# Second attention of a two-layer block: where TensorE's unread products stand, and how wide they are

## The reference

```python
def _L1_xattn_ref(q, k, v, gamma):          # q = layernorm(x), k = v = ctx, all [32, 64, 256]
    qh = q.reshape(B, 8, 8, 256)            # the 64 rows are split in 8 heads of 8 rows
    kh = k.reshape(B, 8, 8, 256)
    vh = v.reshape(B, 8, 8, 256)
    qk = jnp.einsum('bhdq,bhdl->bhql', qh, kh) * scale      # 256 x 256 scores for each head
    sm = jax.nn.softmax(qk, axis=-1)
    ret = jnp.einsum('bhql,bhdl->bhdq', sm, vh)
    return gamma * ret.reshape(B, 64, 256)
x = x + tanh(g_xattn[1]) * _L1_xattn_ref(layernorm(x), ctx, ctx, gamma)
```

## Time and profile before

| what | value |
|---|---|
| median of 3 runs | 708.63 us (707.40 to 709.66) |
| profiled execution: own time, span | 710.47 us, 708.7 us |
| PE busy over the span | 626.2 us (88%) |
| DVE, ACT, POOL busy | 501.0, 422.5, 283.4 us (71%, 60%, 40%) |
| PE in 360 to 370 us, inside the 15 steps | 9.59 of 10 us busy, granted clock 1.00 |

### The profile page before, as it was taken

One profiled execution on the slowest core, in us unless ns is written; L12 is line 12 of the kernel. 1 busy time (PEld: TensorE's weight loads), 2 busy tenths in 40 slices (PEclk: granted clock), 3 DMA queues, 4 the chain that ended last, 5 costly groups with the idle time before them and its releaser, 6 DMA issues. The chain is left out here.

```text
span 708.7 us, 16712 instructions
## 1 busy us (share of the span) xinstructions
PE 626.2 (88%) x5047; PEld 456.8 (64%) x5047; DVE 501.0 (71%) x885; ACT 422.5 (60%) x859; POOL 283.4 (40%) x385
## 2 busy tenths in 40 slices
PE   3788869999999758999999999999859889999995
PEld 2676747788888655444444444444457779999874
DVE  3878784788887965788888888788427744444656
ACT  3888864434343513888888888888825325555430
POOL 2455544222223453444434443453243624214254
PEclk9999987999999965999999999999959979999998
DMA  5444449000000043344333443342000236546444
GB/s 157 113 111 127 132 141 324 19 1 1 0 0 21 4 137 107 96 114 129 112 104 107 122 118 108 101 120 60 2 0 33 93 103 193 162 128 193 120 135 126
DMA packets 70369, 70.42 MB, mean 99 GB/s; under 512 B 10420, under 2 KB 66580, under 8 KB 70324
## 3 DMA queue, kind: packets, MB, share of 16 engines
q1 hardware_dynamic: 65092, 55.55, 26.7%
q0 software_dynamic: 5232, 14.29, 6.7%
HBM read 38.22 MB, written 31.33 MB: 98 GB/s over the span
## 5 line engine op out<-in xcount | busy, mean ns | idle before, releaser
L1375 DVE TENSOR_REDUCE a_smax<-a_s 128x4 f32<-128x1024 f32 x128 | 153.7, 1208 | 38.9 <-PE a_s L1307 37.6
L1189 ACT ACTIVATE a_prob<-a_st 128x512 f32<-128x512 f32 x256 | 144.1, 596 | 38.8 <-PE a_st L1302 37.5
L1302 PEld LDWEIGHTS a_st<-qop,kop 25*128 25x128 f32 x512 | 60.9, 185 | 71.3 <-issue 54.8
L1307 PE MATMUL a_s<-kop,qop 24*128 24x256 f32 x512 | 99.9, 339 | 7.4 <-DVE a_smax L1375 5.0
L1302 PE MATMUL a_st<-qop,kop 25*128 25x256 f32 x512 | 100.3, 330 | 6.6 <-ACT a_prob L1189 5.7
L1246 PE MATMUL a_pv<-a_prob,a_vt 128*32 128x256 f32 x1024 | 81.6, 391 | 2.2 <-ACT a_pv_sb L1174 0.7
L806 POOL TENSOR_TENSOR f_hs_lo<-f_kept,f_hs_hi 128x512 fp32r<-128x512 f32 x32 | 41.3, 1323 | 89.1 <-ACT f_hs_hi L756 89.1
L1307 PEld LDWEIGHTS a_s<-kop,qop 24*128 24x128 f32 x512 | 60.3, 190 | 9.8 <-DVE a_smax L1375 6.3
L1820 POOL DMA_INDIRECT sorted_rows<-m_xn,m_slot x32 | 32.9, 1029 | 49.5 <-PE m_gu L126 26.7
L124 PE MATMUL f_bank<-f_xt_hi,w_hi 128*128 128x512 f32 x128 | 51.6, 403 | 1.1 <-DVE w_raw L849 0.6
L125 PE MATMUL f_bank<-f_xt_lo,w_hi 128*128 128x512 f32 x128 | 50.8, 397 | 0.0
(11 more groups left out here) (260 smaller groups left out, 1700.7 us busy)
## 6 DMA issues: line engine op xcount, KB each, us to landing
kop<-kop_rows SPq DMA_DIRECT2D x128, 48.0 KB
qop<-qop_rows SPq DMA_DIRECT2D x128, 48.0 KB
sorted_rows<-x_all SPq DMA_DIRECT2D x2, 2944.0 KB, 15.4
expert_rows<-turned SPq DMA_DIRECT2D x46, 128.0 KB
kop_rows<-k_hi SPq DMA_DIRECT2D x32, 128.0 KB, 2.3
qop_rows<-q_hi POOLq DMA_DIRECT2D x30, 128.0 KB, 2.4
qop<-sorted_rows SPq DMA_DIRECT2D x24, 128.0 KB, 2.2
kop<-sorted_rows SPq DMA_DIRECT2D x22, 128.0 KB, 2.5
```

Source lines behind the costliest of these rows:

```text
L1189: act.activation(prob[:, u % 8], st_ps[u % 2][:], ACT.Exp, scale=SCALE1).then_inc(prob_ready, 1)
L1302: st = pe.matmul(st_ps[u % 2][:, c * D:(c + 1) * D], lhsT=kop[t.slot][strip, u // 4, c * P:(c + 1) * P], rhs=qop[t.slot][strip, u // 4], s ...
L1307: sm = pe.matmul(s_ps[j % 2][:, k, c * D:(c + 1) * D], lhsT=qop[v.slot][strip, w // 4, c * P:(c + 1) * P], rhs=kop[v.slot][strip, w // 4], ...
L1375: dve.tensor_reduce(smax[:, v.slot, opposite(2 * j):opposite(2 * j) + 2].rearrange("p u q -> p (u q)"), s_ps[j % 2][:].rearrange("p u (q n ...
```

## The change

Four lone products of 512 columns in each of the 15 steps go. In their place stand one such product, ahead of unit 6 behind its waits, and three pairs of products of 256 columns, each right ahead of two transposes (behind u = 2, 11 and 14), behind the waits of these transposes. The pairs write `misc[:, 256:512]`, the half that `selected` fills at u = 8 and ACT copies before u = 11. The number of unread columns of a step stays 4 x 512 = 2048 = 512 + 6 x 256.

```diff
-        EVERY = 4
+        SPARE = 6
...
-                def spare(u):
-
-                    pe.matmul(s_ps[j % 2][:, 0], lhsT=kop[v.slot][:, u // 4, 0:P],
-                              rhs=kop[v.slot][:, u // 8 * 2:u // 8 * 2 + 2].rearrange("p g n -> p (g n)"), start=True, stop=True)
+                def spare(count=2):
+
+                    if v.inside(TILES) and t.inside(TILES):
+                        for g in range(count):
+                            pe.matmul(misc[:, D:2 * D], lhsT=kop[v.slot][:, g % 2, 0:P], rhs=kop[v.slot][:, g % 2], start=True, stop=True)
+
+                def spare_scores():
+
+                    if v.inside(TILES) and t.inside(TILES):
+                        pe.matmul(s_ps[j % 2][:, 0], lhsT=kop[v.slot][:, 0, 0:P],
+                                  rhs=kop[v.slot][:, 0:2].rearrange("p g n -> p (g n)"), start=True, stop=True)
...
-                    if v.inside(TILES) and t.inside(TILES) and u % EVERY == 0:
-                        spare(u)
+                    if u == SPARE:
+                        spare_scores()
...
                     if u == 2:
-                        turn(t, 1, lambda: after(pe, vt_ready, t))
+                        def before():
+                            after(pe, vt_ready, t)
+                            spare()
+                        turn(t, 1, before)
...
                             after(pe, neg_t_ready, t, 2)
                             after(pe, back_ready, o)
+                            spare()
                         turn(v, 0, before)
...
                             pe.wait_ge(vt_cleared, 2)
+                        spare()
                         for c in range(DC):
                             mm = pe.transpose(misc[:, c * P:(c + 1) * P], ctx_t[:, v.slot, c * P:(c + 1) * P], ident[:])
```

## The result

The changed kernel takes 710.09 us (median of 11 executions, 708.72 to 710.80), the kernel before, in the same comparison, 708.27 us (11 executions): ratio 1.0023, 95% interval 1.0014 to 1.0033. It is 1.8 us slower, where 2.4 us less was forecast. Both ratios lie within the 0.3% that the prediction called no change, and both intervals exclude a gain. Three executions that spent far more time at the lower clock than the rest of their kernel (728.09 us of the kernel before, 798.15 us of e6_none, 723.40 us of e8_u12_only) are left out of the ratios.

The account below looks back on a forecast made before the run. PE was taken as the longest engine, each step a chain of its work and ACT's turn-around. Steps of 14.23 against 14.37 us save 2.1 us, the first step 0.3 more: 706.2 us from 708.63, range 702.5 to 711.5.

Parts of the forecast that it names:

- section 1: Transposes at u = 11, or the pair ahead of them, to unit 14: from 1.81 to 2.05 us, +0.24.
- A pair therefore costs 2 x 0.12 = 0.24 beside transposes: PE's price for each new pair beside transposes: 0.24 us, or at most 0.43 if it paid its own change.
- sign of being wrong towards slower: In PE's timeline, a pair with its transposes at over 0.65 us in place of 0.55.
- The sum: Four sections of a step add up to 14.23 us against 14.37, so -0.14 a step.
- sections 3 and 1: Section 3 is unit 2 to unit 6: from 3.44 to 3.68 us, +0.24; section 1 has its own line.
- section 2: Unit 14 to unit 2 of the next step: from 3.50 to 3.31 us, -0.19.
- The delay on ACT: At u = 11, ACT's work queued behind the transposes moves by 0.24 us; neg_t copied 0.66 behind the pair's first product.
- The clock phases in other stages, which I take as unchanged: Outside the changed stage, clock phases stay; they account for 1 us either way.
- No change to speak of: Rival, chance 0.18: small term errors use up the step's saving of 0.14 us; 707.5 to 709.5 us.
- The pairs pay their own change: Rival, chance 0.15: each of three pairs costs 0.19 to 0.20 us more; +0.44 a step, 715.2 us.
- The clock falls: Rival, chance 0.05: PE's clock falls between unit 6 and u = 11; 2 us a fall, 738 us if every step.
- PE's work is what counts: Rival, chance 0.15: ACT's turn-around shrinks and PE's whole saving of 0.38 us a step comes; 702.9 us.

Follow-up runs that it names:

- e6_none: Changed kernel without any unread product in the steps, except the 18 in the first; 702.66 us, ratio 0.9781 to the kernel before.
- e8_u12_only: Kernel before with only the lone product at u = 12 left of its four; 705.46 us, ratio 0.9799.
- e3_behind: Changed kernel with three products of 512 columns right behind the transposes instead of the pairs ahead; 705.20 us, ratio 0.9947 to the kernel before.
- e4_narrow: Changed kernel with 8 columns of weights instead of 128 in the six products beside the transposes; 706.39 us, ratio 0.9968 to the kernel before.
- e9: Changed kernel without the pairs, with products of 512 columns ahead of units 6 and 12; 698.08 us, ratio 0.9846 to the kernel before.
- e5: Changed kernel without its six products of 256 columns, the one ahead of unit 6 kept; 707.00 us, ratio 0.9846 to the kernel before.
- e7_behind_no6: e3_behind without the product ahead of unit 6; 709.96 us, ratio 0.9876 to the kernel before.

## Why the prediction was wrong

- **The frame was right.** A step is a chain of PE's own work and ACT's turn-around. Walked with the price of 0.24, it gives 1.81, 3.31, 3.68 and 5.19 for e3_behind, where the products stand so that 0.24 is their price; measured are 1.81, 3.30, 3.67 and 5.18. The sections measured in the changed kernel are at most 0.08 off, that of section 1 in part by luck, as shown above.
- **The step that failed is "A pair therefore costs 2 x 0.12 = 0.24 beside transposes".** It cost 0.34 ahead of those at u = 2 and u = 11, and 0.27 at u = 14. The prediction priced "beside" from a product that stands behind transposes (u = 12) and from products in a row that was running already. Both rows were true; neither had the product first behind the units' strips, where, by the reading that e4_narrow supports, its weight load of 189 ns lies open instead of the transposes' 84 ns. The price lies between the prediction's bounds of 0.24 and 0.43. The prediction's own sign of being wrong towards slower, a pair with its transposes at over 0.65, is just reached: 0.65 and 0.66 (366.31 to 366.96, 389.21 to 389.87).
- **The sum** was off by +0.16 a step, 2.3 us of the 4.2 between forecast and result: +0.08 and +0.05 in sections 3 and 1, whose transposes load 8 columns, +0.03 in section 2, whose transposes load 128. The forecast gain was 0.14 a step, so a tenth of a microsecond in one price took it all. The 0.3 us more that the first step was to bring did not come: from the stage's first score product to the first context transposes of the 15 steps it is 31.9 and 31.6 us in the profiles of before, 31.8 and 31.6 in the changed ones.
- **The delay on ACT** (section 1) was forecast and came: the pair ahead of the transposes moves the copies behind them, and pv (2, 0) waits 0.36. Its terms were off: the copy of neg_t comes at 0.84 (0.76 in every other step), not at 0.66, and the exponential 0.54 behind it, not 0.66 (0.28 + 0.38), because the 0.38 had been a wait for unit 12. e3_behind gets 0.29 of section 1 back.
- **"The clock phases in other stages, which I take as unchanged"** failed too: the changed kernel's executions spend 3.5 us more at the lower level on average. How much of the 1.4 us that the steps don't explain is due to it, what about the change brings it, and where, stays open.
- **The rivals.** "No change to speak of" is what the steps did. "The pairs pay their own change" did in part: 0.10 of 0.19 each at u = 2 and u = 11, 0.03 at u = 14. "The clock falls" did not happen inside the steps in either profile (granted clock 1.00 from 285 to 505 us). "PE's work is what counts" would have been right for e3_behind alone: 0.38 a step, the same figure, though by another way, since its section 1 is not delayed.
- **On the weight loads** the Trainium skill ("TensorE: Matmul & The Clock Gate", Part 3, The mechanism) has loads overlap matmuls only where row groups differ. In this narrow form (its queue text also allows the background weight buffer) the measurement decides against it here: whole-array loads do lie beside running whole-array products (256 columns each 0.12). What shows as a cost is the first load behind the units' products in strips of the array.

## What to carry to other kernels

A filler product that is to share a change of array shape with useful work belongs behind that work, not ahead of it: ahead, its weight load and its columns delay every engine that waits for the useful result, here 0.4 us a step. Price a filler by its place in the chain: the same 512 columns cost PE 0.43 in front of a unit and 0.24 behind transposes, and a step nothing where the other engine's turn-around is last anyway (e8, e9). The one in front of unit 6 costs a step 0.31 (e5 against e6) or 0.38 (e3 against e7), not its whole 0.43. And when a change is worth a tenth of a microsecond a step, bound each price by a row with the same neighbours on both sides.

## What the runs showed of the hardware that was not expected

- The clock can stay low under full load: in e7_behind_no6 it fell while PE was 5.46 of 6 us busy, and stayed at half for 23 us in which PE had no idle time in the records; without any filler in the steps, behind the 18 that open the first of them, one of four executions took 96 us more than the rest (e6_none).
- A weight load of 8 columns takes 84 ns, one of 128 columns 189 ns, and the 0.10 us between them shows in the chain where such a load is the first of a group behind another shape of the array (e4_narrow against the changed kernel).
- The time at the lower clock differs between executions of one kernel: in e4_narrow from 66 us (702.0 to 702.2 us in all) to 89 us (710.0 us), with the same code and data, and one us of it costs less than the half that the two levels suggest: 0.30 us in e4_narrow, 0.12 in the kernel before.
